# Moving ScalarE's copies of the transposes of x behind the exponentials, and VectorE's low parts of them behind its other work

## The reference, cut to what matters

```python
# x: (64, 128, 256), ctx: (64, 128, 192); 16 heads of 64
n = layernorm(x)
q = n @ Wq + lora(n);  k, v = ctx[:, :124] @ Wk + lora, ctx[:, :124] @ Wv + lora
k_ipa, v_ipa = ctx[:, 124:] @ Wk_ipa, ctx[:, 124:] @ Wv_ipa
o = softmax(q k^T / 8) v + softmax(q k_ipa^T / 8) v_ipa
x = x + o @ Wo + bo + lora(o)
# feed-forward: 8-bit activations, ternary weights, a depthwise convolution over 3 tokens
h = bit_linear(layernorm(x), w1);  h = silu(conv1d(h) + conv_b)
out = x + bit_linear(h, w2)
```

## Time and profile before

| | |
|---|---|
| time, median of 3 runs | 1582.96 us (1582.52 to 1586.33) |
| profiled execution, its own time | 1581.49 us |
| its span, first to last instruction | 1579.7 us |
| mean granted TensorE clock | 0.976 |
| PE busy | 1447.4 us (92%) |
| DVE busy | 1218.0 us (77%) |
| ACT busy | 1178.2 us (75%) |
| POOL busy | 648.4 us (41%) |

### The profile page before, as it was taken

How to read it: one execution, slowest core, us unless ns; L and a number is a source line. 1 busy time by engine, 2 the same in 40 slices (tenths; PEclk the granted TensorE clock), 3 DMA queues, 4 the chain that set the end, 5 groups by cost and what they waited for, 6 DMA issues and landing times.

```text
span 1579.7 us, 33324 instructions
## 1 busy us (share of the span) xinstructions
PE 1447.4 (92%) x10732; PEld 1178.4 (75%) x10778; DVE 1218.0 (77%) x3061; ACT 1178.2 (75%) x3909; POOL 648.4 (41%) x1053
## 2 busy tenths in 40 slices
PE   6999999999999999999999999999999999999742
PEld 3778878787787878787787878778787878777521
DVE  4254688787969888787978878787987879686966
ACT  2477896978878797887879697887879788786721
POOL 0134443544444344444444354444434444444500
PEclk9899999999999999999999999999999999999965
DMA  7400001000010100000010000001010000000000
GB/s 198 123 30 16 30 16 30 16 28 29 14 42 14 42 0 27 29 27 29 14 42 14 29 14 27 29 14 42 14 42 0 27 29 27 29 1 28 1 14 13
DMA packets 41128, 47.13 MB, mean 30 GB/s; under 512 B 3008, under 2 KB 35200, under 8 KB 41088
## 3 DMA queue, kind: packets, MB, share of 16 engines
q1 hardware_dynamic: 40032, 45.82, 9.4%
q10 hardware_dynamic: 1056, 0.81, 0.2%
HBM read 36.13 MB, written 10.49 MB: 30 GB/s over the span
## 4 chain that ended last, share of the span: by engine, by line
PE 52%; ACT 19%; DVE 18%; issue 9%; DMA 0%; DVEq 0%; POOL 0%; ACTq 0%; POOLq 0%
PE PS L462 10%; ACT SM L650 8%; PE PS L424 7%; PE PS L475 6%; PE PS L405 5%; PE PS L440 5%; PE PS L449 4%; PE PS L414 4%; PE PS L523 3%; ACT HP L671 2%; DVE GBS L865 2%; PE PS L502 2%; DVE GBS L886 2%; ACT GBS L676 2%; ACT QM L617 1%
## 5 line engine op out<-in xcount | busy, mean ns | idle before, releaser
L1025 POOL TENSOR_TENSOR SM<-SM,RC 128x496 f32<-128x496 f32 (+1 forms) x512 | 331.6, 668 | 748.6 <-DVE RC L800 748.6
L650 ACT ACTIVATE SM<-PS,MX 128x124 f32<-128x124 f32 x1024 | 358.7, 365 | 147.1 <-DVE SM L806 145.0
L462 PE MATMUL PS<-KT,QM 128*128 128x128 f32 x2048 | 277.4, 278 | 29.6 <-ACT SM L650 29.4
L462 PEld LDWEIGHTS PS<-KT,QM 128*128 128x128 f32 x2048 | 248.8, 192 | 45.2 <-ACT SM L650 44.5
L650 ACT ACTIVATION_READ_ACCUMULATOR SM<-PS,MX 128x1 f32 x1024 | 212.7, 208 | 0.0
L1051 POOL TENSOR_TENSOR OTl<-OF,OTh 128x256 fp32r<-128x256 f32 x256 | 196.6, 768 | 14.5 <-ACT OF L644 14.5
L642 ACT ACTIVATE OTh<-PS 128x256 fp32r<-128x256 f32 x256 | 100.3, 392 | 116.1 <-PE PS L440 114.9
L449 PE MATMUL PS<-IDF,SM 128*128 128x128 f32 x1024 | 168.4, 287 | 8.2 <-POOL SM L1025 8.1
L804 DVE TENSOR_REDUCE MX<-PS 128x4 f32<-128x496 f32 x256 | 170.2, 665 | 0.0
L440 PE MATMUL PS<-PT,V 128*64 128x128 f32 x2048 | 168.8, 286 | 0.1
L440 PEld LDWEIGHTS PS<-PT,V 128*64 128x64 f32 x2048 | 106.8, 136 | 82.0 <-issue 75.0
(11 more groups left out here) (139 smaller groups left out, 3576.4 us busy)
## 6 DMA issues: line engine op xcount, KB each, us to landing
XIN<-in_x SPq DMA_DIRECT2D x16, 512.0 KB, 3.6
XRES<-in_x SPq DMA_DIRECT2D x16, 512.0 KB, 3.5
out_y<-HP SPq DMA_DIRECT2D x16, 512.0 KB, 3.0
CRAW<-in_ctxT SPq DMA_DIRECT2D x16, 256.0 KB, 2.7
RRAW<-in_ctxT SPq DMA_DIRECT2D x32, 128.0 KB, 2.8
QM<-in_Wq SPq DMA_DIRECT2D x1, 1024.0 KB, 11.0
GBS<-in_Wo SPq DMA_DIRECT2D x1, 1024.0 KB, 21.1
k_ipa_columns<-HP SPq DMA_DIRECT2D x1, 1024.0 KB, 5.1
```

What stands on the lines that cost most here:

```text
L462: m = mm(psS[:, h, :], QM[:, 2 * q + h // 2, h % 2, TOK * b:TOK * b + TOK], KT[:, 2 * q + h // 2, b, :], start=True, stop=True)
L650: m = act.activation(SM[s % 2][:, h, 0:ORG], psS[:, h, 0:ORG], ACT.Exp, bias=MX[s % 2][:, h:h + 1], accum_out=SU[s % 2][:, h:h + 1])
L1025: m = pool.tensor_tensor(part, part, RC[c % 2][:, 4 * i:4 * i + 4].unsqueeze(2).broadcast_to(shape), ALU.mult)
```

## The change

ScalarE's two copies from the transposes' banks (L611) move from half 8 to half 9. As the exponentials of a step stand at the end of the even half, the copies come behind the exponentials of step 4. VectorE's two low parts stay in half 9, but become a function of their own, `x_low`, that is called last in the half, behind `finish`. Nothing is added or taken away.

```diff
-                if n == N_XT:
+                if n == N_XT + 1:
                     for k in range(2):
                         act.wait_ge(unit_full, g.count(UNITS, k + 1))
                         act.activation(XT[0][:, k, :], psU[k], ACT.Identity).then_inc(xt_high, 1)
...
-                if n == N_XT + 1:
-                    for k in range(2):
-                        dve.wait_ge(xt_high, g.count(2, k + 1))
-                        dve.tensor_tensor(XT[1][:, k, :], psU[k], XT[0][:, k, :].bitcast(F32), ALU.subtract).then_inc(unit_free[k], 1)
...
+            def x_low(g, n):
+                if n == N_XT + 1:
+                    for k in range(2):
+                        dve.wait_ge(xt_high, g.count(2, k + 1))
+                        dve.tensor_tensor(XT[1][:, k, :], psU[k], XT[0][:, k, :].bitcast(F32), ALU.subtract).then_inc(unit_free[k], 1)
...
             for n in range(EARLY_HALVES):
                 project(At(0), n)
+                x_low(At(0), n)
...
                     project(g.shift(1), n)
                 if g.shift(-1).exists():
                     finish(g.shift(-1), n)
+                if g.shift(1).exists(1):
+                    x_low(g.shift(1), n)
```

## The result

The changed kernel takes 1608.58 us (median of 4 runs, 1606.92 to 1611.69), the kernel before 1582.74 us in the runs beside it. The ratio is 1.0158, with a 95% interval of 1.0141 to 1.0175. I had said 1607, between 1597 and 1622. The profiled execution took 1606.92 us with a span of 1605.1 us; its mean granted clock is 0.970 where it was 0.976.

A forecast was written before the change was run, and what follows sets the result against it. It took a chain handed between engines as the bound, through VectorE's stretch and then TensorE. A TensorE stall of 14 x 1.34 = 18.8 us plus 6 us of lower clock gave 25 us over 1583, said as 1607, range 1597 to 1622.

The forecast's parts named there:

- What bounds the kernel: No engine alone; in steps 4 to 6 the chain runs through VectorE's gapless stretch, with TensorE beside it having little slack.
- ScalarE, cost 0 and gain 0: Step 4's exponentials and step 5's scores come about 0.97 us earlier, but VectorE gains nothing; group 0's pass taken as 0.
- VectorE, XTl 2.55 us later, nothing behind it moved: Low parts of x start at 635.39 behind normalisation and largest values; the next instruction still starts at 636.59.
- TensorE's stall: First Q matmul waits for VectorE's low parts: 1.74 us late plus 0.10 restart, 1.84 us; idling some 2.6 us a pass.
- Net 1.34 us a pass: Delay at step 6's scores: 1.84 less slacks of 0.06 and 0.34 and a saved restart of 0.10; 18.8 us in 14 passes.
- The clock: TensorE's new gaps are followed by falls to 1.2 GHz in 4 to 5 of 14 passes, 1.3 us each, 6 us.
- I take nearer to the low end: Choice of 4 to 5 falls between 0 and 14, the gap being only about 0.6 us over 2.00 and followed by dense matmuls.
- Sum: Stall 18.8 us plus clock 6 us, 25 us in all; 1608 against the median, 1606.5 against the profiled execution, said as 1607.
- The rivals: Stall alone 1602 (0.16), falls in nearly all passes 1623 (0.17), stall hidden 1583 (0.05), faster 1569 (0.04).
- The stall alone: TensorE waits at the Q projection but its clock never falls: 1583 + 19 = 1602 us; chance 0.16.
- Falls in all 14 passes: Clock falls in nearly every pass after TensorE's gap, 14 x 1.5 = 21 us on top of the stall: 1623; chance 0.17.

The follow-up runs named there:

- run 1: Changed kernel with ScalarE's copies of x back in half 8, so only VectorE's low parts of x stay moved; 1599.18 us against 1584.47 for the kernel before.
- run 2: Kernel before with only ScalarE's copies of x moved behind the exponentials of step 4; 1583.15 us against 1584.47.
- run 6: Kernel before with VectorE's normalisation and largest values one half later, behind the maxima of step 5; 1584.70 us against 1584.38.
- run 4: Changed kernel plus 10 unused TensorE matmuls before the Q projection's wait in the passes of groups 1 to 14; 1598.15 us against 1584.47 for the kernel before.
- run 9: Changed kernel with VectorE's low parts of x behind the maxima of step 5, plus 14 unused matmuls in TensorE's gap; 1619.26 us against 1582.47 before.
- run 10: Kernel before with normalisation, largest values and later feed-forward one half later, scales and rounding behind the maxima of step 6; 1628.87 us against 1583.48.
- run 11: Kernel before with normalisation, scales, rounding and later feed-forward moved later, plus ScalarE's copies of x behind step 4's exponentials; 1627.10 us against 1583.48.
- run 8: Changed kernel with VectorE's low parts of x later still, behind the maxima of step 5; 1646.91 us against 1584.38 for the kernel before.
- run 5: Changed kernel plus 2 unused TensorE matmuls at the start of its idling in the passes of groups 1 to 14; 1607.44 us against 1584.38 before.
- run 3: Changed kernel with VectorE's low parts of x between the normalisation and the largest values; 1581.77 us against 1584.47 for the kernel before.
- run 12: Kernel before with ScalarE's copies moved, normalisation, scales and rounding later, and feed-forward tiles two halves later (M_F1 17); 1587.37 us against 1582.47.
- run 7: Kernel before with normalisation and largest values one half later and ScalarE's copies of x behind the exponentials of step 4; 1584.87 us against 1584.38.

## Why the prediction was right

- *What bounds the kernel.* That the chain runs through VectorE's stretch, whose inner order is free, and that TensorE runs beside it with little slack, was right: run 1 and run 2 separate the two. That little slack was left in VectorE's strand too was seen only in run 6.
- *ScalarE, cost 0 and gain 0.* Right (run 2), but for group 0's pass, where it gained 0.6 us (I had taken 0, within 1), and but for one side effect that I didn't name as ScalarE's: by taking the first wait away it made one long gap of two short ones.
- *VectorE, XTl 2.55 us later, nothing behind it moved.* Right to 0.01 us.
- *TensorE's stall.* 2.56 us of idling where I had about 2.6 to 2.7. The restart cost 0.10 us (459.17 to 459.50 against 0.235), and TensorE's weight loads waited for the same result, 38.8 us in 15 waits by the list of waits of PEld:

```profile
PEld PS L405 <- DVE XTl L794: 38.8, 15, 2.8
```

So the rule of the Trainium skill, "TensorE: Matmul & The Clock Gate" (Part 2), by which weight loads can be pulled ahead of running matmuls, saved nothing at this wait; the row was the better guide.
- *Net 1.34 us a pass.* Measured 1.20. The mis-sized term is the slack before the scores of step 6. I took the 0.34 us of the bracket. By the starts, the scores came 639.30 - 638.31 = 0.99 us behind the transposes where they need 0.50 (463.02 - 462.52 above), so the slack was 0.49: 1.84 - 0.06 - 0.49 - 0.10 = 1.19. The Trainium skill, "Perfetto Trace Analysis" (Per-engine timelines), says that TensorE's end times are estimated and not observed; the bracket is counted from such an end, and the starts agree with the measured time, the bracket doesn't.
- *The clock.* The mechanism was right and in the sum (runs 4 and 9). Its size was off: 8 falls in the profiled execution for my 4 to 5, 12.5 us for my 6. The step that failed is "I take nearer to the low end": I had no row that said how the number of falls grows with the gap. And I had overlooked what my own stretch from 1469.48 to 1473 held. TensorE's timeline of the kernel before has there

```profile
1473.44 1.03 PE L502 MATMUL PS<-Q1T,W 128*128 128x512 bf16 x2 [2.55 <-DVE GBS L865]
```

That is a gap as long as the new one, behind one of 0.80 us. It was followed by a fall and by dense matmuls. This gap returns near the end of every profiled execution here but those of runs 10 and 11, 2.54 to 2.55 us long, and the clock fell at it in all twelve. So a gap of this length with matmuls right behind it was no case without a precedent. A fall's cost was 1.3 to 1.6 us as taken from the rows, but one lasted twice as long.
- *Sum.* 14 x 1.2 = 17 us and 12.5 of clock, 29, would have given 1612. The median came out at 1608.6, and the profiled execution was helped by 3.0 us in the preparation ahead of the loop, where its clock happened to be low for a shorter time. That my 1607 is so near is in part luck, as errors cancel: stall too large by 2, clock too small by 6, the preparation not in the sum. How many falls the other three executions had no trace shows.
- *The rivals.* The stall alone would have been about 1599 (runs 1 and 4); it lay 9 us below. Falls in all 14 passes happened only in run 8, with gaps of 3.35 us and more. The advice in the closing table of the Trainium skill, "TensorE: Matmul & The Clock Gate", is against idle gaps that are longer than this one. By it the clock would have stayed up, and this case contradicts it: the clock fell in 8 passes with gaps of 2.34 and 2.56 us, and in 6 of run 5 with 1.89 and 2.12.

## What to carry to other kernels

An operation that stands in the critical chain only because its engine works in order can be moved inside its stretch, but its own consumer has a date too: find the first instruction that needs the result, add up what will stand ahead, and compare with the consumer's slack, read from starts and not from brackets. Here about 0.6 us of lateness, the restart included, was free, and each microsecond beyond it cost one in every pass, until the gap was long enough to cost the clock as well. A wait taken away from TensorE ahead of another wait doesn't shorten its idling, it merges it. If a long wait can't be avoided, matmuls in it whose results nobody uses can be worth their while.

## What the runs showed of the hardware

TensorE's granted clock against its idling at the Q projection, by the profiled executions (14 passes each, stretches of 0.25 us over the whole loop). In pass 1 the gap is 0.2 to 0.4 us shorter than in the others:

| run | idle us, pass 1 | idle us, the others | passes with a fall to 1.2 GHz | us |
|---|---|---|---|---|
| 4, filled | 0.17 | 0.40 | 0 | 1598.15 |
| 9, low parts last, filled | 0.32 | 0.70 (pass 2: 0.93) | 0 | 1619.26 |
| 3, low parts earlier | 1.09 | 1.32 | 0 | 1581.77 |
| 1, VectorE's part alone | 1.33 | 1.56 (and 0.95 before) | 0 | 1599.18 |
| 5, filled in part | 1.89 | 2.12 | 6, pass 1 among them | 1607.44 |
| the changed kernel | 2.34 | 2.56 | 8, pass 1 among them | 1608.58 |
| 8, low parts last | 3.35 | 3.72 to 3.97 | 14 | 1646.91 |

I had not expected falls at 2.1 us to be nearly as frequent as at 2.6, nor that a fall would come in some passes and not in others of the same kernel, whose work is the same to 0.01 us. The length of a gap alone doesn't decide it. Near the end of run 10 TensorE idled 3.00 us, and the clock stayed at 2.4 GHz before and behind it, in its timeline:

```profile
1494.28 1.13 PE L493 MATMUL PS<-IDF,AD 128*128 128x128 f32 x8 [3.00 <-ACT Q1T L658]
```

At the same instruction of run 11 a gap of 2.99 us was followed by a fall, and in run 12 one of 3.00 wasn't. So it was with gaps of 2.13 us in run 6 (no fall) and 2.12 in run 7 (a fall). Why it differs these runs don't settle.

Nor had I expected a low clock in the preparation that lasts 10 us in one execution and 3.4 in another, with TensorE busy all the time (10.20 of 10.20 us in the stretch above). Group 0's mark came at 101.2 to 101.6 us in the five profiled executions with 3.4 us of low clock there or none, at 103.4 to 103.6 in six with 6.8, and at 104.2 to 104.3 in the two with 10.2; run 12, whose mark came at 105.1 with 3.4 us, had begun 3 us later.
